# A gated attention and quantised feed-forward layer on one core: one rotation sum moved between DVE and Pool, the first unit's maxima started in the last batch of projections, the last residual summed half by Pool

## The reference

```python
q, k, v = proj(layernorm(x), Wq, bq), proj(ctx, Wk, bk), proj(ctx, Wv, bv)
q = q * cos + rotate_half(q) * sin
k = k * cos + rotate_half(k) * sin
out = softmax(q @ k.T * scale) @ v            # per batch and head
x = x + tanh(g_xattn) * (out @ Wo.T + bo)
xq = fake_quant(layernorm(x), clip_x)         # one scale for the whole tensor
h = fake_quant(silu(xq @ Wg.T) * (xq @ Wu.T), clip_down)   # one scale again
x = x + tanh(g_ffn) * (h @ Wd.T)
```

## Time and profile before

| | us |
|---|---|
| median of 3 runs | 588.55 |
| lowest, highest | 588.35, 588.63 |
| the profiled execution, whole | 589.7 |
| its span, first to last instruction | 587.8 |
| projections | 0 to 105.3 |
| attention, prologue | 105.3 to 120.2 |
| attention, loop and end | 120.2 to 500.5 |
| feed-forward, up to the second scale | 500.5 to 556 |
| down stage | 556 to 587.8 |

### The profile page before, as it was taken

The page is one execution under the profiler, slowest core; times in us unless marked ns, Lnnn a source line. Parts: engine busy times, 40 slices in busy tenths (PEclk is TensorE's granted clock), DMA queues, the critical chain, the costliest instruction groups (busy, mean ns, idle before and its releaser), DMA issues. The chain is left out here.

```text
span 587.8 us, 18041 instructions
## 1 busy us (share of the span) xinstructions
PE 564.7 (96%) x6579; PEld 265.2 (45%) x6584; DVE 531.4 (90%) x684; ACT 444.8 (76%) x874; POOL 241.1 (41%) x366
## 2 busy tenths in 40 slices
PE   9999999999999999999999999999999999999985
PEld 4555655234344444444444444444444533544364
DVE  3999999999999999999899899899899885699988
ACT  2667776267787897897897897798799673799694
POOL 2799999701310335453224214215214211366400
PEclk9999999999999999999999999999999999999999
DMA  8579864422212222221231122122121000000024
GB/s 272 186 239 349 286 221 158 135 89 91 69 60 77 79 65 56 76 84 54 59 100 58 54 84 78 54 70 92 55 56 55 3 2 1 2 1 1 1 108 178
DMA packets 29902, 55.21 MB, mean 94 GB/s; under 512 B 5544, under 2 KB 19752, under 8 KB 29864
## 3 DMA queue, kind: packets, MB, share of 16 engines
q1 hardware_dynamic: 29864, 54.71, 29.0%
HBM read 37.62 MB, written 16.78 MB: 93 GB/s over the span
## 5 line engine op out<-in xcount | busy, mean ns | idle before, releaser
L929 ACT ACTIVATE prob<-st_ps 128x512 f32<-128x512 f32 x512 | 280.7, 596 | 61.6 <-PE st_ps L787 54.4
L787 PE MATMUL st_ps<-q,k 98*32 98x512 bf16 x2048 | 178.3, 380 | 1.9 <-ACT prob L929 1.9
L989 DVE TENSOR_REDUCE negm<-xT_ps 128x2 f32<-128x1024 f32 x128 | 154.5, 1207 | 7.3 <-PE xT_ps L339 6.8
L989 DVE TENSOR_REDUCE negm<-v_ps 128x2 f32<-128x1024 f32 x128 | 154.3, 1205 | 3.8 <-PE v_ps L339 3.8
L811 PE MATMUL pv_ps<-prob,v_u 128*32 128x512 f32 x1024 | 132.5, 592 | 0.6 <-ACT prob L929 0.3
L787 PEld LDWEIGHTS st_ps<-q,k 98*32 98x32 bf16 x2048 | 57.0, 95 | 90.8 <-ACT prob L929 34.0
L1181 POOL TENSOR_TENSOR msplit<-negm,onesf 128x16 bf16<-128x16 f32 x32 | 7.1, 221 | 205.8 <-DVE negm L989 205.8
L339 PE MATMUL xT_ps<-k,q 96*32 96x512 bf16 x1024 | 78.4, 379 | 1.1 <-DVE negm L989 1.0
L339 PE MATMUL v_ps<-k,q 96*32 96x512 bf16 x1024 | 78.1, 380 | 1.3 <-DVE negm L989 0.9
L339 PEld LDWEIGHTS xT_ps<-k,q 96*32 96x32 bf16 x1024 | 27.0, 96 | 36.6 <-issue 12.9
L811 PEld LDWEIGHTS pv_ps<-prob,v_u 128*32 128x32 f32 x1024 | 31.1, 110 | 26.8 <-issue 2.8
(11 more groups left out here) (149 smaller groups left out, 786.5 us busy)
## 6 DMA issues: line engine op xcount, KB each, us to landing
qk_parts<-parts SPq DMA_DIRECT2D x32, 384.0 KB, 3.2
k<-qk_parts SPq DMA_DIRECT2D x32, 192.0 KB
q<-qk_parts SPq DMA_DIRECT2D x32, 192.0 KB
ctx<-in_ctxT SPq DMA_DIRECT2D x8, 512.0 KB, 4.7
X<-in_x SPq DMA_DIRECT2D x8, 512.0 KB, 6.4
k<-qk_parts SPq DMA_DIRECT2D x32, 128.0 KB
q<-qk_parts SPq DMA_DIRECT2D x32, 128.0 KB
out<-X SPq DMA_DIRECT2D x7, 512.0 KB, 2.6
```

The costliest lines, as they stand in the source:

```text
L787: last = nc.tensor.matmul(score_bank(i)[lo:lo + COLS, :], k6[g][:, h, kt * P + lo:kt * P + lo + COLS], q6[g][:, h, :], start=True, stop=True)
L929: nc.scalar.activation(prob[kt % 2][:, h, :], score_bank(HPU * kt + h)[:], ACT.Exp, scale=SCALE).then_inc(exp_done, 1)
L989: nc.vector.tensor_reduce(negm[g % 2][:, lo:lo + 2], pair[:], op=ALU.max, axis=AX.X, negate=True).then_inc(mx_read, 1)
```

## The change

1. **Sums of the rotation.** Pool's sum 1 becomes DVE's and DVE's sum 3 becomes Pool's. In each batch Pool now does lo 0, sums 2 and 3, lo 1 to 3, sum 0, and then `scale_and_shift`; DVE does the rests 2 and 3 with two statistics between, and its sum 1 between rope 1 and rest 0. The last batch keeps sum 1 on Pool.
2. **Maxima of unit 0 begun early.** `negm` and the semaphore move to where the first block can use them. In the last batch PE makes score pair 0 ahead of q and pair 1 between the two halves of q, and pairs 2 to 4 at the end of the block. DVE takes maxima 0 and 1 ahead of and behind rest 0, rope 2, then maxima 2 and 3. Its rest 1 goes to Pool in the second block, its rope 3 to the second block between maxima 7 of unit 0 and maxima 0 of unit 1. Pool does there, after the values of unit 0: lo 0, sum 2, rest 1, the split of unit 0, rest 2, sum 3, rest 3, lo 1 to 3. SP issues the row maxima and the load of unit 3 ahead of the four stores of the last batch.
3. **Residual.** Of each of the chunks 0 to 6 DVE sums the first two tiles of four and Pool the other two; of the last chunk Pool sums the first two and DVE the last two. `scale_out(n)` waits for Pool's half of chunk n-2, and each send waits for both engines.

```diff
+        AHEAD = 4
@@ PE, first block
+                    if is_last(b):
+                        pe.wait_ge(unit_in[0], NLOAD)
+                        pe.wait_ge(xnT_ready, KC * B)
+                        query_scores(0, 0, 0, mx_ps[0])
                     for m in range(2):
...
+                        if is_last(b) and m == 0:
+                            pe.wait_ge(v_kept, 2 * B)
+                            query_scores(0, 0, 1, mx_ps[1])
...
-                pe.wait_ge(unit_in[0], NLOAD)
-                pe.wait_ge(xnT_ready, KC * B)
-                query_scores(0, 0, 0, mx_ps[0])
-                pe.wait_ge(v_kept, 2 * B)
-                query_scores(0, 0, 1, mx_ps[1])
+                for n in range(2, AHEAD + 1):
+                    pe.wait_ge(mx_read, n - 1)
+                    query_scores(0, n // 2, n % 2, mx_ps[n % 2])
@@ DVE, first block
-                        rope_sum(dve, nc.vector, b - 1, 3)
+                        rest_part(dve, nc.vector, b - 1, 2)
                         if ahead:
                             statistics(b + 2, (2, 3))
-                        for i in (2, 3):
-                            rest_part(dve, nc.vector, b - 1, i)
+                        rest_part(dve, nc.vector, b - 1, 3)
...
+                    if not is_last(b):
+                        rope_sum(dve, nc.vector, b, 1)
...
                     for i in (0, 1):
-                        rest_part(dve, nc.vector, b, i)
+                        if is_last(b):
+                            maxima(dve, 0, 0, 0, i, mx_ps[i])
+                        if not (is_last(b) and i):
+                            rest_part(dve, nc.vector, b, i)
...
-                for i in (2, 3):
-                    rope(dve, B - 1, i)
+                rope(dve, B - 1, 2)
+                for n in range(2, AHEAD):
+                    maxima(dve, 0, 0, n // 2, n % 2, mx_ps[n % 2])
@@ Pool, first block
                         lo_part(pool, b - 1, 0)
-                        rope_sum(pool, nc.gpsimd, b - 1, 2)
+                        for i in (2, 3):
+                            rope_sum(pool, nc.gpsimd, b - 1, i)
                         for i in (1, 2, 3):
                             lo_part(pool, b - 1, i)
-                    for i in (0, 1):
-                        rope_sum(pool, nc.gpsimd, b, i)
+                    rope_sum(pool, nc.gpsimd, b, 0)
+                    if is_last(b):
+                        rope_sum(pool, nc.gpsimd, b, 1)
@@ down stage
+        def residual(eng, ns, n, t0, done, summed):
+
+            eng.wait_ge(y1_ready, done)
+            x = X[:, 4 * n + t0:4 * n + t0 + 2, :]
+            ns.tensor_tensor(x, y1[n % 2][:, t0:t0 + 2, :], x, ALU.add).then_inc(summed, 1)
...
+                    if n >= 2:
+                        dve.wait_ge(sum_pool, n - 1)
...
-                        residual(n - 1, 0, 4, n)
+                        residual(dve, nc.vector, n - 1, 0, n, sum_dve)
...
+                for n in range(NCH):
+                    residual(pool, nc.gpsimd, n, 2 if n < NCH - 1 else 0, n + 1, sum_pool)
```

More of the change, by code:

```diff
@@ L208, in build @@
         cs = sb(mid, "cs", [P, 2, S])
+        negm = [sb(mid, f"negm{i}", [P, HPU * TPB]) for i in range(2)]
         stA = ExitStack()
@@ L341, in query_scores, with maxima @@
             last.then_inc(mx_ready, 1)
+        def maxima(dve, b, g, h, j, pair):
+            dve.wait_ge(mx_ready, 8 * (UPB * b + g) + 2 * h + j + 1)
+            lo = h * TPB + 2 * j
+            nc.vector.tensor_reduce(negm[g % 2][:, lo:lo + 2], pair[:], op=ALU.max, axis=AX.X, negate=True).then_inc(mx_read, 1)
+        AHEAD = 4
         CONSTS = 5
@@ L474, in _ @@
                     body(0, odd)
-                with pe.Fori(1, B // 2) as pair:
+                with pe.Fori(1, B // 2 - 1) as pair:
                     for odd in range(2):
                         body(pair, odd)
+                for odd in range(2):
+                    body(B // 2 - 1, odd)
                 pe.wait_ge(rot_ready, 4 * (B - 1) + 2)
@@ L765, in _ @@
                 load_unit(sp, 0, 2)
-                for i in range(3):
+                max_rows(0, 0)
+                load_unit(sp, 0, 3)
+                for i in range(4):
                     store(sp, B - 1, i)
-                max_rows(0, 0)
-                store(sp, B - 1, 3)
-                load_unit(sp, 0, 3)
                 for i in range(4):
@@ L906, in _ @@
                         for j in range(2):
-                            if (g or h) and not (g and h == HPU - 1):
+                            if 8 * g + 2 * h + j > AHEAD and not (g and h == HPU - 1):
                                 pe.wait_ge(mx_read, 8 * g + 2 * h + j - 1)
                                 query_scores(g, h, j, mx_ps[j])
-                                stay_busy(st_ps[(TURN_SLOT + 1) % 3][:], PROLOGUE)
+                                stay_busy(st_ps[1][:], PROLOGUE)
                         if g and h == 0:
                             max_transpose(0, -1)
+                pe.wait_ge(rot_ready, 4 * B)
                 over_batches(pe, body, B, True)
@@ L964, in body @@
                                 take_max(b, g)
[L965 to L970, removed]
+                mid_part(act, B - 1, 0)
+                hi_part(act, B - 1, 2)
+                mid_part(act, B - 1, 1)
                 take_max(0, -1)
+                mid_part(act, B - 1, 2)
+                hi_part(act, B - 1, 3)
+                mid_part(act, B - 1, 3)
                 body(0)
@@ L984, in _ @@
             def _(dve):
[L985 to L989, removed]
                 def turn_out(b, g):
@@ L1127, in keep_weights @@
                     last.then_inc(wT_kept, 1)
[L1129 to L1135, removed]
+                for n in range(AHEAD, 8):
+                    maxima(dve, 0, 0, n // 2, n % 2, mx_ps[n % 2])
+                rope(dve, B - 1, 3)
+                for n in range(6):
+                    maxima(dve, 0, 1, n // 2, n % 2, mx_ps[n % 2])
                 body(0)
@@ L1255, in _ @@
                 unit_values(0, 0)
+                lo_part(pool, B - 1, 0)
+                rope_sum(pool, nc.gpsimd, B - 1, 2)
+                rest_part(pool, nc.gpsimd, B - 1, 1)
                 split_max(0, 0)
+                rest_part(pool, nc.gpsimd, B - 1, 2)
+                rope_sum(pool, nc.gpsimd, B - 1, 3)
+                rest_part(pool, nc.gpsimd, B - 1, 3)
+                for i in (1, 2, 3):
+                    lo_part(pool, B - 1, i)
                 pool.wait_ge(wobv_kept, 1)
@@ L1339, in build @@
         y1_ready = sem("y1_ready")
-        out_ready = sem("out_ready")
+        sum_dve = sem("sum_dve")
+        sum_pool = sem("sum_pool")
         out_done = sem("out_done")
@@ L1631, in _ @@
                     if n:
-                        residual(n - 1, 0, 4, n)
+                        residual(dve, nc.vector, n - 1, 0, n, sum_dve)
                 for i in range(2):
                     scale_out(NCH - 1, 2 * i, 2 * i + 2)
-                for i in range(2):
-                    residual(NCH - 1, 2 * i, 2 * i + 2, NCH + i)
+                residual(dve, nc.vector, NCH - 1, 2, NCH + 1, sum_dve)
             @block.gpsimd
@@ L1648, in _, with send @@
                 out_v = out_dram
-                def send(t0, t1, ready):
-                    sp.wait_ge(out_ready, ready)
+                def send(t0, t1):
                     sp.dma_start(out_v[:, t0:t1, :], X[:, t0:t1, :]).then_inc(out_done, DMA)
                 for n in range(NCH - 1):
-                    send(4 * n, 4 * n + 4, n + 1)
-                for i in range(2):
-                    send(4 * (NCH - 1) + 2 * i, 4 * (NCH - 1) + 2 * i + 2, NCH + i)
+                    sp.wait_ge(sum_dve, n + 1)
+                    sp.wait_ge(sum_pool, n + 1)
+                    send(4 * n, 4 * n + 4)
+                sp.wait_ge(sum_pool, NCH)
+                send(4 * NCH - 4, 4 * NCH - 2)
+                sp.wait_ge(sum_dve, NCH)
+                send(4 * NCH - 2, 4 * NCH)
                 sp.wait_ge(out_done, (NCH + 1) * DMA)
```

30 lines of the change are left out of this document (9 added, 21 removed).

## The result

The changed kernel takes **591.63 us**, the median of 6 runs (590.65 to 592.59); the kernel before, run beside it, 588.59 us (588.35 to 589.35, 6 runs). The ratio is 1.0047, with a 95% interval of 1.0037 to 1.0058: slower by 2.2 to 3.4 us. The forecast was 591.5. The profiled execution took 591.45 us, its span 589.4.

What follows compares the result with a forecast made beforehand. A two-batch loop through DVE, Pool, ACT and PE bounds the projections, DVE the down stage. Profiled: 589.7 - 0.9 - 0.5 + 4.3 = 592.6 us; median: 588.55 + 2.9 = 591.5 us; 8-in-10 range 587.6 to 593.2.

Steps and rivals of the forecast that it cites:

- The bound of the down stage and the hold: Down stage: Pool's residual half holds DVE 1.2 us, chunk goes from 3.2 to 3.86 us, +4.3 us in all.
- The lower bound of that term: Down stage: without any hold DVE's chunk is 2.66 us and ACT becomes the limit, -1.6 us.
- xn stands in the same place against the rests: Projections: x_rstd follows DVE's rests as before, so the early shift gives nothing; period 11.57 us, 0.2 less.
- rival B: Front: PE alone sets the period, pair 2 not late, -2.5 - 1.0; tail +3.0; 588.05 us, probability 0.14.
- The wait for maxima 2: Seam: DVE waits a new 0.9 us, since PE makes pair 2 only behind q, fillers and four matmuls.
- ACT, SP and Pool in the prologue: Start of attention: their moved steps are not late; ACT or SP coming late was the +1.0 us bound.
- Rival A: Down stage: Pool's half is hidden under scale_out and the stage gives 1.6 us; 585.5 us, probability 0.16.
- Rival C: Front gives nothing, DVE held in rest 2 and by x_rstd ahead of rest 1: 594 us, probability 0.08.

Runs made afterwards that it cites:

- kernel with 4 columns: Changed kernel, but Pool adds only 4 of the 256 columns of its residual tiles, all semaphores and waits kept: 585.93 us, ratio 0.9954.

## Why the prediction was right, and where it was off

The forecast was +2.9 us and the measured difference +3.0; the terms below, by stages, add up to some +2.6, within the interval of 2.2 to 3.4.

- **The bound of the down stage and the hold (part 3, forecast +4.3, measured +3.95).** The mechanism is as written: DVE is held for the length of Pool's instruction and scale_out is not. Two sizes were off. A hold is 1.07 to 1.09 us (1.75 to 1.77 less the 0.68 of a free half) and not 1.2: DVE ends 0.55 us behind Pool where a free half takes 0.68. And it falls on all seven chunks (in the first on a clip, 1.70 us for two that take 0.62), where I left 0 to 0.65 open for the last. From start to start the seven chunks cost 0.54 to 0.57 us each, 3.88 together, and the last halves 0.07. The chunk was forecast at 3.86 us, and is 3.69 and 3.83.
- **The lower bound of that term, -1.6 for no hold, did not go far enough.** The kernel with 4 columns is 2.7 us shorter in the stage. ACT gives the 0.8 us that I counted, but behind its last scaling there are 1.9 us less (576.28 to 580.01, where it was 579.68 to 585.31) and not 0.6: chunk 6's residual shrinks too, by 0.54, and scale_out(6) starts 0.24 us ahead of ACT's end instead of 0.67 behind it.
- **Part 1 (forecast -0.9, measured -1.0: -1.4 in the projections, +0.4 at the seam).** The sum came out by luck, through two errors that cancel. The period is 11.48 us and not 11.57, because x_rstd does not follow rest 1 as before but is already asking when it ends; so the step "xn stands in the same place against the rests" failed, by 0.3 us, and PE alone sets the period, which was rival B's mechanism at a smaller price. PE alone needs 11.48 us and not 11.42 or less, so that nothing is left beyond it. The holds were placed less well than their sum: rest 2 is held 1.07 us and not 0.7 (1.75 us where I wrote about 1.2), rest 3 0.18 and not 0.3, the sum 1 0.06 and not 0.4, 1.31 us together against 1.4. The 0.4 us at the seam I had not seen: in the last batch, where Pool keeps sum 1, DVE has the cost of sum 3 on Pool without the gain.
- **Part 2 (forecast -0.5, measured -0.4).** The wait for maxima 2 is there, but 0.45 us and not 0.9. I had carried over what PE needed before from its fillers to the next pair, 1.73 us (101.97 to 103.70), in which the product for the bias starts as Pool's factors are done (100.94 + 1.65 = 102.59); in the changed kernel it follows the fillers at once, and it is 1.39 us (100.78 to 102.17). Instead there are two more waits, 0.36 us for q and 0.39 for maxima 5, where PE's four fillers at the head of the second block stand in front of pair 5. The first I had counted at 0.25, the last not. The new waits are 1.20 us together where the forecast had 1.15, so this term too is right by errors that cancel. What it did not have at all is the lower clock of one run in four.
- **ACT, SP and Pool in the prologue** are not late, as forecast: the attention stage behind the first weight maximum takes 432.5 us in every kernel.
- **Rival A** is refuted where the change puts Pool's half; its mechanism, Pool's work under scale_out, is there where the experiment holds the half back. **Rival C** did not happen: rest 2 is held 1.07 us, x_rstd never comes ahead of rest 1.

## What to carry to other kernels

Before giving half of an elementwise step to Pool, list what DVE does in the time that Pool's half will take. If these are sums with two SBUF inputs or clips like those here, DVE is held for nearly the whole of Pool's instruction and saves half of its own, here 1.07 us for 0.54. The same half is worth having when it is held back to lie beside a DVE instruction that reads PSUM, here 1.5 us less than before the change (27.85 against 29.39) for one wait on a semaphore that was there. And when work is moved so that PE waits at another place, look at the granted clock of every timed run: the 0.90 us that PE waits here went with a lower clock in 11 of 46 runs, and it shows in the mean clock of a run before it shows in a median.

## What the runs showed beyond what was expected

- Memset on Pool leaves a two-input sum on DVE untouched (0.68 us beside 0.93), and holds two clips (1.34 us instead of 0.62).
- In the contest with DVE, Pool came first in all seven chunks, although DVE's next instruction had no wait to make; in four of them Pool was itself held by a clip (1.38 us against 1.27) and still came ahead of what followed the clip.
- The first rotation starts between 9.15 and 11.12 us by the landing of the first loads, for the same list of transfers. Two profiles should be lined up behind this mark before stages are compared.
